# A perceiver block on one core: keys laid out for attention inside SBUF, and batch 0 prepared alone first

## The reference, cut to what matters

```python
def _xattn(Q, K, V, mask, Wq, bq, Wk, bk, Wv, bv, Wo, bo):     # 16 heads of 8
    q = (Q @ Wq.T + bq).reshape(B, Sq, 16, 8).transpose(0, 2, 1, 3)
    k = (K @ Wk.T + bk).reshape(B, Sk, 16, 8).transpose(0, 2, 1, 3)
    v = (V @ Wv.T + bv).reshape(B, Sk, 16, 8).transpose(0, 2, 1, 3)
    attn = softmax(einsum('bhqd,bhkd->bhqk', q, k) / sqrt(8) + mask, axis=-1)
    return einsum('bhqk,bhkd->bhqd', attn, v)...reshape(B, Sq, 128) @ Wo.T + bo

x = x + _xattn(layernorm(x), ctx, ctx, mask, ...)   # x: 4 x 128 x 128, ctx: 4 x 2048 x 128
x = x + _ssm(layernorm(x), ...)                     # needs the spectral norms of W_in, W_out
x = x + _ffn(layernorm(x), ...)                     # weights w1, w2 replaced by mean(|w|) * sign(w)
```

## Time and profile before

| | us |
|---|---|
| median of 3 runs (lowest to highest) | 327.06 (324.84 to 327.69) |
| the profiled execution: its time | 329.18 |
| the profiled execution: span, first to last instruction | 327.4 |
| TensorE busy / VectorE / ScalarE / GpSimd | 257.0 / 231.3 / 200.7 / 108.2 |
| mean granted TensorE clock | 0.895 of full speed |

### The profile page before, as it was taken

One profiled execution on the slowest core, in us unless ns is written; L12 is line 12 of the kernel. 1 busy time (PEld: TensorE's weight loads), 2 busy tenths in 40 slices (PEclk: granted clock), 3 DMA queues, 4 the chain that ended last, 5 costly groups with the idle time before them and its releaser, 6 DMA issues.

```text
span 327.4 us, 9590 instructions
## 1 busy us (share of the span) xinstructions
PE 257.0 (79%) x3904; PEld 160.6 (49%) x3904; DVE 231.3 (71%) x425; ACT 200.7 (61%) x309; POOL 108.2 (33%) x267
## 2 busy tenths in 40 slices
PE   0799615499999999999999999999999877550276
PEld 0577401245555556555565655555655444440156
DVE  4358839267878788787878989879888940538941
ACT  1267700267777777877777777777876665195042
POOL 7123421115434553345433665232113120104210
PEclk9999955569999999999999999999999996785559
DMA  6926979941535415344263312311321000000001
GB/s 146 381 88 220 226 179 292 363 153 50 148 92 153 146 50 161 107 127 145 52 188 102 103 50 77 73 50 50 80 68 52 3 4 2 0 0 0 0 0 32
DMA packets 24565, 34.48 MB, mean 105 GB/s; under 512 B 2444, under 2 KB 19112, under 8 KB 24392
## 3 DMA queue, kind: packets, MB, share of 16 engines
q1 hardware_dynamic: 23716, 33.37, 35.0%
q0 software_dynamic: 128, 0.14, 0.5%
q10 hardware_dynamic: 676, 0.33, 0.3%
HBM read 20.20 MB, written 13.63 MB: 103 GB/s over the span
## 4 chain that ended last, share of the span: by engine, by line
PE 58%; ACT 17%; SPq 6%; DMA 6%; DVE 6%; issue 5%; POOL 2%; POOLq 0%; ACTq 0%; DVEq 0%
PE ps L447 15%; ACT probs L739 13%; PE ps L434 13%; PE ps L418 6%; PE ps L320 4%; PE ps L357 4%; SPq L259 4%; PE ps L487 3%; PE ps L495 3%; DMA k_rows_dram<-k_parts 2%; DMA w_kv<-in_L_xattn_Wq_dram 2%; PE ps L455 2%; PE ps L667 2%; PE ps L340 2%; DMA ctx_buf<-in_ctx_dram 1%
## 5 line engine op out<-in xcount | busy, mean ns | idle before, releaser
L1191 DVE TENSOR_REDUCE pmax<-ps 128x2 f32<-128x1024 f32 x128 | 156.1, 1224 | 42.8 <-PE ps L418 41.0
L739 ACT ACTIVATE probs<-ps 128x1024 f32<-128x1024 f32 x128 | 130.8, 1022 | 47.2 <-PE ps L434 47.2
L447 PE MATMUL ps<-probs,v_now 128*9 128x128 f32 x2048 | 82.4, 280 | 0.2 <-ACT probs L739 0.2
L434 PE MATMUL ps<-q_max,k_rows 51*128 51x128 bf16 x1024 | 52.3, 223 | 13.9 <-ACT probs L739 12.8
L447 PEld LDWEIGHTS ps<-probs,v_now 128*9 128x9 f32 x2048 | 43.8, 91 | 34.9 <-issue 33.1
L418 PE MATMUL ps<-k_rows,q_now 48*128 48x512 bf16 x256 | 51.2, 398 | 11.0 <-DMA k_rows<-k_rows_dram 8.3
L968 POOL CAST max_cols<-negmax 128x2 bf16<-128x2 f32 x32 | 6.1, 192 | 133.6 <-DVE negmax L1197 133.6
L434 PEld LDWEIGHTS ps<-q_max,k_rows 51*128 51x128 bf16 x1024 | 30.0, 96 | 37.5 <-ACT probs L739 22.7
L418 PEld LDWEIGHTS ps<-k_rows,q_now 48*128 48x128 bf16 x256 | 12.8, 96 | 14.2 <-DMA k_rows<-k_rows_dram 8.5
L690 ACT ACTIVATE ctxT<-ps 128x512 f32<-128x512 f32 x16 | 9.6, 597 | 14.2 <-PE ps L320 14.2
L357 PE MATMUL ps<-power 128*128 128x128 f32 x96 | 16.7, 297 | 0.2 <-DVE power L1119 0.2
(11 more groups left out here) (184 smaller groups left out, 360.0 us busy)
## 6 DMA issues: line engine op xcount, KB each, us to landing
k_rows<-k_rows_dram SPq DMA_DIRECT2D x64, 192.0 KB, 3.3
k_rows_dram<-k_parts SPq DMA_DIRECT2D x16, 384.0 KB, 3.8
ctx_buf<-in_ctx_dram SPq DMA_DIRECT2D x16, 256.0 KB, 5.5
k_rows_dram<-k_parts SPq DMA_DIRECT2D x16, 256.0 KB, 3.7
k_rows_dram<-k_parts SPq DMA_DIRECT2D x16, 128.0 KB, 4.1
mask_sb<-in_mask_1x1xSxS_ff_dram SPq DMA_DIRECT2D x1, 1024.0 KB, 9.3
q_all<-q_rows_dram SPq DMA_DIRECT2D x2, 384.0 KB, 6.5
w_nat<-in_L_ffn_w_dram SPq DMA_DIRECT2D x2, 256.0 KB, 8.8
```

What stands on the lines that cost most here:

```text
L434: t = pe.matmul(dst, k_rows[rows, i % 4, at:at + P], q_max[rows, i % 2, :], start=not masked, stop=True, skip_group_check=masked)
L447: t = pe.matmul(ps[at:at + HEAD_COLS, 6, 0:P], v_now[:, i % 2, 4 * c + j, HEAD_COLS * h:HEAD_COLS * h + HEAD_COLS], probs[:, c, h, P * j:P ...
L739: act.activation(probs[:, u % CHUNKS, :, :], ps[:, 4:6, :], ACT.Exp).then_inc(probs_ready, 1)
L1191: dve.tensor_reduce(pmax[:, i % 2, :, c], ps[:, bank:bank + 2, :], AX.X, ALU.max).then_inc(pmax_ready, 1)
```

## The change

- **Key rows.** `store_k` and the DRAM buffer go. `load_half_pair` copies each half's rows from `k_parts` (8 partitions, one for each component of the head) to 56 rows of `k_rows` with three DMAs inside SBUF. A part is repeated whole, so there are seven products in place of six, and a pair takes six DMAs in place of two. Queries go through DRAM as before, in the new order of rows, batch 0 first.
- **Prologue.** Chunks 0 to 3 (batch 0) are turned and projected first, with ctxT and k_32 in four slots; chunk 4 behind them; chunks 5 to 7 between the first `scores` of the loop (`early_chunk`). The layer norm and query split of batch 0 come ahead of those of the others. On GpSimd the root for batches 1 to 3 (`rest_root`) stands between `third(1)` and `third(2)`; its four DMAs come after `third(3)`. Half 1 of pair 0 is loaded on ScalarE's queue.
- **Side steps.** Keys of a chunk are projected whole at step 2, values whole at step 4. Steps 3 and 6 are empty. The Gram matrices are made at step 7 of chunk 14.
- **Squarings.** All 24 are in units 64 to 111, four in each group of eight (steps 0, 2, 3, 4), with weights turned at step 6 of groups 0, 1, 3 and 4.
- **Copies.** `q_now` and `v_now` go: `scores` and `pv` read `q_all` and `v_all`. `weight_means` and `weight_signs` move on VectorE from the prologue to units 42 and 44.

```diff
-    EARLY_SQUARES = 6
+    RAY_UNITS = SQUARE_UNITS + 2 * SQUARINGS
+    EARLY, CTX_SLOTS, SQ_PERIOD = CHUNKS, 6, 4
-    LOADS = 32
+    LOADS = 16 * 6
+        def load_half_pair(eng, i, h):
+            b, p = divmod(i, PAIRS)
+            at, slot = HALF_ROWS * h, i % 4
+            heads = slice(16 * p + HD * h, 16 * p + HD * h + HD)
+            keys = slice(KEYS * b, KEYS * b + KEYS)
+            for rows, parts in ((slice(at, at + TRIPLE), PARTS), (slice(at + TRIPLE, at + 2 * TRIPLE), PARTS),
+                                (slice(at + 2 * TRIPLE, at + ROWS), 1)):
+                eng.dma_start(k_rows[rows, slot, :], k_parts[heads, 0:parts, keys]).then_inc(k_rows_loaded[slot], 16)
...
+            def early_chunk(n):
+                pe.wait_ge(ctxT_ready, n)
+                turn_ctx(7, n)
+                pe.wait_ge(k32_ready, n - EARLY)
+                project_k(6, n)
+                wait(pe, v_ready, n - 1)
+                project_v(4 + n % 2, n)
             def attend(masked):
-                for u in range(6):
-                    scores(u, masked)
+                scores(0, masked)
+                scores(1, masked)
+                pe.matmul(ps[:, 7, T:TOK], kvT[:, 2, :], xnT[:, T:TOK], start=True, stop=True)
+                scores(2, masked)
+                pe.wait_ge(once("q_step"), 5)
+                early_chunk(5)
+                scores(3, masked)
+                early_chunk(6)
+                scores(4, masked)
+                early_chunk(7)
+                scores(5, masked)
...
             def side_prep(n, at, i):
-                elif at in (2, 3):
-                    half = slice(256 * (at - 2), 256 * (at - 2) + 256)
-                    pe.matmul(ps[:, 7, half], kvT[:, 0, :], ctxT[:, n % 2, half], start=True, stop=True)
+                elif at == 2:
+                    side_taken(i)
+                    pe.matmul(ps[:, 7, :], kvT[:, 0, :], ctxT[:, n % EARLY, :], start=True, stop=True)
-                elif at in (4, 6):
-                    for j in range(at - 4, at - 2):
+                elif at == 4:
+                    pe.wait_ge(k32_ready, n - EARLY + 1)
+                    project_v(7, n)
...
             def side_squares(g, i):
                 elif at == 2:
                     side_taken(i)
-                    square(7, k + 1)
+                    square(k + 1)
+                elif at == 3:
+                    square(k + 2)
                 elif at == 4:
-                    square(7, k + 2)
+                    square(k + 3)
...
-            for n in range(FIRST):
-                third(n)
+            third(0)
+            third(1)
+            rest_root()
+            third(2)
+            third(3)
```

More of the change, by code:

```diff
@@ L241, in _ @@
             load_ctx(0)
[L242 to L247, removed]
+            sp.dma_start(w_kv[:, 0, :], Wk).then_inc(ld["wk"], 16)
+            for n in range(1, EARLY):
                 load_ctx(n)
+            sp.dma_start(w_kv[:, 1, :], Wv).then_inc(ld["wv"], 16)
@@ L249, in _ @@
             sp.dma_start(mask_sb[:, :], mask.rearrange("a b q k -> (a b q) k")).then_inc(ld["mask"], 16)
[L250 to L261, removed]
+            for n in range(EARLY, CTX_SLOTS):
+                load_ctx(n)
@@ L278, in _ @@
-            store_k(0)
-            store_k(1)
+                    load_half_pair(sp, i, h)
+            first_tokens, rest_tokens = slice(0, T), slice(T, TOK)
             sp.wait_ge(once("q_parts_ready"), 1)
[L281 to L284, removed]
+            store_q(sp, first_tokens)
@@ L285, in _ @@
+            for n in range(CTX_SLOTS, FIRST):
+                load_ctx(n)
             sp.wait_ge(once("q_stored"), 16 * 3)
@@ L320, in turn @@
                 return pe.transpose(dst, src, ident[:, :])
[L323 to L327, removed]
             def turn_ctx(bank, n):
-                pe.wait_ge(ctx_loaded[n % FIRST], 16 * (n // FIRST) + 16)
+                pe.wait_ge(ctx_loaded[n % CTX_SLOTS], 16 * (n // CTX_SLOTS) + 16)
@@ L388, in _, with turn_xn @@
-            project_k(FIRST - 1)
-            project_v(FIRST - 1)
-            sum_norms(EARLY_SQUARES // SQ_PERIOD)
-            pe.wait_ge(once("q_step"), 1)
-            pe.wait_ge(once("mask_abs_ready"), 1)
-            turn(ps[0:1, 1, 0:P], mask_abs[:, 0:1]).then_inc(once("mask_turned"), 1)
+            def turn_xn(first, n):
+                for i in range(first, first + n):
+                    t = turn(ps[:, 3, P * i:P * i + P], xn[:, i, :])
+                t.then_inc(once("xn_turned"), 1)
@@ new lines, in _ @@
+            turn_ctx(1, 3)
+            pe.wait_ge(r1_ready, 1)
+            project_k(4, 2)
+            pe.wait_ge(ld["wq"], 16)
+            turn(ps[:, 2, P:2 * P], w_kv[:, 2, :])
+            pe.wait_ge(ld["wv"], 16)
+            turn(ps[:, 2, 2 * P:3 * P], w_kv[:, 1, :]).then_inc(once("qv_turned"), 1)
+            pe.wait_ge(once("xn_ready"), 1)
+            turn_xn(0, 1)
+            pe.wait_ge(r1_ready, 2)
+            project_k(5, 3)
+            pe.wait_ge(once("qT_ready"), 2)
+            pe.matmul(ps[:, 2, 0:P], kvT[:, 2, :], xnT[:, 0:T], start=True, stop=True).then_inc(once("q_done"), 1)
@@ L417, in scores @@
                     rows = slice(HALF_ROWS * h, HALF_ROWS * h + ROWS)
-                    t = pe.matmul(ps[:, bank + h, :], q_now[rows, i % 4, :],
+                    t = pe.matmul(ps[:, bank + h, :], q_all[rows, i % PAIRS, i // PAIRS, :],
                                   k_rows[rows, i % 4, 512 * c:512 * c + 512], start=not masked, stop=True)
@@ new lines, in _ @@
+            first_k(0)
+            copy_ctx(0, 2)
+            first_k(1)
+            copy_ctx(1, 3)
+            first_k(2)
+            act.wait_ge(once("qv_turned"), 1)
+            copy(kvT[:, 2, :], ps[:, 2, P:2 * P], once("vec_ready"))
+            copy(kvT[:, 1, :], ps[:, 2, 2 * P:3 * P], once("qT_ready"))
+            act.wait_ge(once("xn_turned"), 1)
+            copy(xnT[:, 0:T], ps[:, 3, 0:T], once("qT_ready"))
+            first_k(3)
+            for n in range(EARLY):
+                take_vall(6 + n % 2, n)
@@ L733, in _ @@
+            act.wait_ge(once("k_ones_ready"), 1)
+            act.wait_ge(k3_ready, EARLY)
+            load_half_pair(act, 0, 1)
+            act.wait_ge(once("xn_turned"), 2)
+            copy(xnT[:, T:TOK], ps[:, 3, T:TOK], once("qT_ready"))
+            for n in range(EARLY, FIRST):
+                copy_ctx(7, n)
+                whole_k(6, n)
+                take_vall(4 + n % 2, n)
             act.wait_ge(ld["rows"], 16 * 4)
@@ L1141, in _ @@
[L1141 to L1150 removed]
+            rest_k(0)
+            rest_k(1)
+            rest_k(2)
+            split_q_first(2, first_tokens, 0)
+            rest_k(3)
+            split_q(first_tokens, 0)
+            split_q_rest(first_tokens, 0)
```

593 lines of the change are left out of this document (282 added, 311 removed).

## The result

The changed kernel takes 370.0 us (368.7 to 371.1), the kernel before 326.1 beside it: 1.134 times as long, 95% interval 1.127 to 1.142. The forecast was 325.0, the range 315 to 360: wrong in sign and outside the range. It went as rival A described, and further.

A forecast was written before the change was run, and what follows sets the result against it. It saw TensorE waiting at the start and, in the loop, each unit limited by the larger of two chains. Terms -11.3 + 7.0 + 0.4 + 1.4 + 0.4 = -2.1 gave 327.1 us profiled, median 325.0; range 315 to 360.

The forecast's parts named there:

- rival A: Key-row loads: reads from 8 partitions starve the loop, 8.1 us a pair, median 356 us; chance 0.27.
- (6): Removed copies, 56-row matmuls and later key-row loads in the loop: no cost, loads of 6.3 us a pair hidden.
- the power law: Key-row loads: rate falling with partitions touched, carried on from 128 and 48 partitions to 8, gives 57 GB/s.
- (2): First scores to keyscores(2): 23.5 us of work, so keyscores(2) at 55.5, 9.5 earlier; with the clock, gain 11.3 us.
- (1): Prologue up to the first scores: it starts at 32 us (29 to 35), 16 us earlier than before.
- B: Start better than forecast, clock back early, plus exponential slipping ahead in the loop: 317 us; sign, clock 1.00 before 45; chance 0.22.
- C: Start not shortened because GpSimd's queue holds the negated maxima of pair 0, keyscores(0) unmoved: 335 us; chance 0.06.
- (3): Loop, chunk projected in three pieces, not five: eight units take 14.3 us, 0.88 more; eight chunks +7.0, Gram step +0.4.
- (4): Squarings in the loop: six more in empty steps at 0.24 us each, +1.4 us.
- (5): Weight means and signs on VectorE in the loop: +0.4 us, 0 to 1.5; without VectorE's lead all 3.3 would show.

The follow-up runs named there:

- m2_strides: No kernel, only 96 KB copies alone on the chip, from eight source partitions at distance 1, 2, 4, 8, 16: 49, 98, 142, 100, 98 GB/s.
- e2_spread: The changed kernel with a head's eight key components in every fourth partition instead of eight neighbours: 334.6 us, 1.027 of the kernel before.
- e6_start: e5_five_pieces with GpSimd's third(2) and third(3) ahead of rest_root: 320.4 us, 0.982 of the kernel before.
- e5_five_pieces: e4_ctx_first with keys and values of chunks 8 to 15 projected in halves again, as before the change: 323.5 us, 0.990 of the kernel before.
- e4_ctx_first: e2_spread with the loads of context chunks 8 and 9 moved ahead of weights and queries on the SP queue: 326.9 us, 1.001 of the kernel before.
- e8_weights: e6_start with the feed-forward weights' sums and signs on VectorE laid one by one behind single units: 315.2 us, 0.965 of the kernel before.

## Why the prediction was wrong, point by point

**(6) failed, and it decided the result.** The prediction took the later loads as hidden, "3.3 to land", from the loads out of DRAM. Measured: 8.0 us a pair against a loop of 6.7 to 7.2. The step itself named what it rested on, and rival A had the price: 57 GB/s from the power law and 8.1 us a pair; the kernel shows 57 and 8.0. What was wrong is the weight. No row showed a read from few partitions, and a row of another kind of transfer, DRAM to 48 partitions, stood in the sum at full trust. The margin that was needed was a factor of 2.1 (3.3 to 7), and the earlier trace rows had just such a factor between 128 and 48 partitions.

The mechanism that A gave was only partly right. It said "the rate goes with the partitions touched". m2_strides touches eight partitions each time and gets 49 to 142. What the runs showed in its place is the layout: eight neighbours are the worst of the five layouts tried. So it is luck that A's 57 met the kernel's 57. Alone, eight neighbours give 49, and m2_strides suggests that the kernel gets more because its source changes with each half.

**A's time was 356, measured 370.** It had the first `scores` at 32 (34.8), and 5 us for other loads between; the key loads in fact stood from 50.5 to 70.8. The slots were full, and pair 4's came free only with `keyscores(3)` at 70.1. This comes from the failure of step (2). It puts the end of the last key load's issue at 297.3, where A's sum has the last pair at 288: 9 of the 14 us. I have not divided up the rest.

**(1) held in mechanism and was 3 us short.** First `scores` 34.8 for 32. The GpSimd order was as read: root at 20.03, `third(2)` and `third(3)` from 20.86 (22 to 24.8 in the prediction). The loads went out 3 us early, but ScalarE, with its three issues of pair 0 (23.2 to 28.0, 1.6 us each), copied chunk 4 only after 28, so that TensorE was through with it at half clock at 32.9 and not 31, and stood 1.9 us more, marked "issue", whose cause I didn't trace. Slow loads aren't it: e2_spread starts at 35.0. With `third` ahead of the root e6_start has its `scores` at 30.8 and `keyscores(2)` at 54.35, 3.8 earlier than e5_five_pieces.

**(2) failed.** It listed TensorE's work between the first `scores` and `keyscores(2)` and not what the SP queue must do before chunk 8 lands. The diff shows the order: pairs, weights, a wait for the queries, their store, another wait, their loads, and then chunk 8. That is independent of (6): e2_spread, with fast loads, starts `keyscores(2)` at 65.04, no earlier than before, after a wait of 6.9 us for chunk 8, and e4_ctx_first moves it to 57.0. The gain of 11.3 was real work saved, but fell into a wait for a load that was queued too low. The work itself was well sized: from the first `scores` to `keyscores(2)` e4_ctx_first takes 23.2 us for 23.5. B's sign, clock 1.00 before 45 us, did appear (1.00 from 43.5 to 57.2, after 6.8 us at 0.50), without B's gain, as TensorE then ran into that wait. C is out: `keyscores(0)` starts at 53.0, before at 56.3.

**(3) held.** Eight units 14.39 for 14.3, 13.40 before; the steps in e2_spread are 1.69, 1.73, 2.16, 1.82, 2.19, 1.67, 1.61, 1.52 against the eight that the prediction lists. Three pieces cost 0.98 us a chunk for 0.88, 7.8 for eight where the prediction has 7.0. What one step left idle, the next didn't use. One reading was off without harm: the steps before are six near 1.73 and two of 1.52, not seven near 1.70 and one of 1.52; the sum is the same.

**(4) off in nothing that matters.** A group with squarings 13.35 for 13.09 before; over six groups 1.5 us for the 1.4 predicted.

**(5) held in the change and was mis-sized as a rule.** With three pieces the group with the weights takes 15.14 for 14.39, 0.75 us, inside "0 to 1.5". With five pieces the same work costs 4.7 us (45.1 for three groups in e6_start, 40.4 in e8_weights): TensorE runs dry and the clock drops. That it does so because a unit is 0.12 us shorter, so that VectorE makes up less, is argued and not shown. "Without that lead all 3.3 would show" left out the clock.

**Sum.** Without (6) and (2)'s queue, as in e4_ctx_first, the change is 326.9 us for the 325.0 predicted: within its own range, but no gain over the 327.1 beside it. Where the profiled executions come out at -2.2 us, near the forecast's -2.1, part of it is luck. The start gives 8.0 and the loop from `keyscores(2)` takes 8.0 more, and the 2.2 lie behind the last `keyscores`, where the prediction has nothing. There the clock of the kernel before fell at 272.0, ahead of its last `keyscores` (274.0), and that of e4_ctx_first at 279.0, behind it (273.9).

Two things stay open: what the waits of the changed kernel don't cover of its loss in the loop, and what moves the prologue by 1 to 2 us from one profiled execution to another, which is only seen and not explained.

## What to carry to other kernels

A copy's rate must come from a row with the same source layout; if there is none, the range belongs around the slow end. Where one head's data sits in neighbouring partitions, either spread it or alternate copies of distant groups on the queue: the first costs a permutation of the weights, the second nothing. A step moved earlier gains only if every load that it needs is moved with it on its queue. A lump of work on an engine with little spare time can cost more than its length: laid out one by one these operations cost nothing, in one piece 4.7 us, of them 2 us of idle TensorE and the rest while the clock was at half.

## What the runs showed that was not expected

Eight source partitions give 49, 98, 142, 100 and 98 GB/s at distances 1, 2, 4, 8 and 16: more distance isn't better beyond 4, and the 142 is SP's pace of issue and not the path's. At the slow rate the DMA engines show a share of 0.48 and no more, so a share of one half can mean a full path. Copies queued one behind another on the same queue gain when their sources lie in different groups (84 GB/s in turn, 49 from one group). An issue on the SP queue takes 0.65 us for such a copy when nothing is in its way, and 1.14 when the queue is full; so the time of issues tells of the transfers ahead.
